# A guess of ScalarE and one Newton step for the quotients of a recurrence, in a decoder layer on one core

## The reference

```python
x = _layernorm(x + _L0_attn_ref(x, Wqkv, bqkv, Wo, bo))
x = _layernorm(x + _wkv(w, u, k=x, v=ctx))
x = _layernorm(x + _L0_ffn_ref(x, ...))      # (silu(g) * u) @ Wd.T

# _wkv, one step in time, for each batch row and channel
no = jnp.maximum(o, u + kt)
A = jnp.exp(o - no)
E = jnp.exp(u + kt - no)
y = (A * p + E * vt) / (A * q + E)
...
return ((A2 * p + E2 * vt, A2 * q + E2, no2), y)
```

## Time and profile before

| | us |
|---|---|
| three runs | 717.31, 719.03, 719.50 |
| their median | 719.03 |
| span of the profiled execution | 717.3 (the run of 717.31) |
| PE busy | 694.5 (97%) |
| DVE busy | 552.5 (77%) |
| ScalarE busy | 457.5 (64%) |
| GpSimd busy | 314.9 (44%) |

### The profile page before, as it was taken

How to read it: one execution, slowest core, us unless ns; L and a number is a source line. 1 busy time by engine, 2 the same in 40 slices (tenths; PEclk the granted TensorE clock), 3 DMA queues, 4 the chain that set the end, 5 groups by cost and what they waited for, 6 DMA issues and landing times. The chain is left out here.

```text
span 717.3 us, 13042 instructions
## 1 busy us (share of the span) xinstructions
PE 694.5 (97%) x4658; PEld 427.9 (60%) x4658; DVE 552.5 (77%) x1252; ACT 457.5 (64%) x1072; POOL 314.9 (44%) x352
## 2 busy tenths in 40 slices
PE   8899999999999999999999999999999799999997
PEld 3466665666666666656555454544455697578855
DVE  4567666879899988899945899998898786466644
ACT  5689885779887678768756744356552566346620
POOL 2015340455677342442345756576675243203321
PEclk9999999999999999999999999999999999999999
DMA  7846891343243043228026010000001000010001
GB/s 254 265 150 160 241 211 53 110 128 89 81 126 95 24 136 116 55 65 177 2 33 143 1 60 15 30 16 0 1 1 45 16 2 1 1 60 1 1 16 45
DMA packets 45538, 54.24 MB, mean 76 GB/s; under 512 B 4897, under 2 KB 34849, under 8 KB 45473
## 3 DMA queue, kind: packets, MB, share of 16 engines
q1 hardware_dynamic: 41632, 46.59, 21.2%
q0 software_dynamic: 3264, 6.29, 5.3%
q10 hardware_dynamic: 576, 0.52, 0.3%
HBM read 47.10 MB, written 12.58 MB: 83 GB/s over the span
## 5 line engine op out<-in xcount | busy, mean ns | idle before, releaser
L1422 DVE CUSTOM_DVE_ANT_0 ee<-psb,mask,clip 128x512 f32<-128x512 f32 (+3 forms) x256 | 131.1, 536 | 28.9 <-PE psb L974 28.3
L1201 ACT ACTIVATE ee<-ee,nm 128x512 f32<-128x512 f32 (+3 forms) x256 | 143.0, 561 | 1.4 <-DVE nm L1422 1.4
L1813 POOL TENSOR_TENSOR hl<-ring,hh 128x512 f16<-128x512 f32 x64 | 77.3, 1220 | 103.6 <-ACT hh L1315 61.3
L1212 ACT ACTIVATE ee<-psb 128x512 f32<-128x512 f32 (+1 forms) x172 | 87.1, 525 | 38.5 <-PE psb L985 33.4
L985 PE MATMUL psb<-ident,ee 128*128 128x128 f32 x640 | 97.6, 274 | 3.2 <-ACT ee L1212 3.0
L1110 PE MATMUL psb<-wd,hl 128*128 128x512 f16 x240 | 91.0, 379 | 0.6 <-POOL hl L1813 0.6
L1108 PE MATMUL psb<-wd,hh 128*128 128x512 f16 x240 | 91.0, 379 | 0.0
L985 PEld LDWEIGHTS psb<-ident,ee 128*128 128x128 f32 x640 | 75.6, 141 | 24.5 <-ACT ee L1212 6.0
L974 PE MATMUL psb<-ks,qs 128*128 128x512 f16 (+3 forms) x256 | 72.0, 301 | 2.7 <-DVE nm L1422 1.3
L1521 DVE RECIPROCAL ek<-ek 128x128 f32<-128x128 f32 x64 | 58.2, 931 | 6.5 <-POOL ek L1781 6.5
L932 PE MATMUL psb<-xh,wqk 128*128 128x512 f16 x240 | 59.8, 379 | 0.4 <-ACT wqk L1178 0.4
(11 more groups left out here) (205 smaller groups left out, 1614.4 us busy)
## 6 DMA issues: line engine op xcount, KB each, us to landing
qs<-parts SPq DMA_DIRECT2D x64, 128.0 KB, 2.8
ks<-parts SPq DMA_DIRECT2D x60, 128.0 KB, 3.0
parts<-qhl SPq DMA_DIRECT2D x16, 256.0 KB, 2.2
...
```

What stands on the lines that cost most here:

```text
L1201: e.activation(dst, dst, ACT.Exp, bias=NM[:, n % 4, col:col + 1], scale=-1.0, accum_out=DEN[:, n % 4, col:col + 1]).then_inc(sem("exp"), 1)
L1212: e.activation(ET[h][:, base:base + width], PSB[:, bank["turn", H, item], 0:width], ACT.Copy).then_inc(sem("et"), 1)
L1422: e.tensor_tensor_reduce(E[H % 3][:, EOFF[i]:EOFF[i] + w], PSB[:, bank["score", H, i], 0:w], MASK[:, S - w:S], -SC, CLIP[:, i:i + 1], ALU. ...
L1813: e.tensor_tensor(HS[it][1][:], pair(b, it // 2)[:, it % 2, :] if b in SEVEN else ring(b, it)[1], HS[it][0][:], ALU.subtract).then_inc(sem ...
```

## The change

A column has five pieces now, ek apart: scan_q, scan_p, seed, refine, divide.

- `seed`: ScalarE takes the logarithm of the denominator into a new buffer SEED (2 KB for each partition), then the exponential of minus that, in place. Both functions and the exponential of `ek` are in one table set, which `logs()` loads where the gate's function was used since.
- `refine`: GpSimd multiplies the denominator by the seed (r) and the numerator by the seed (s).
- `divide`: DVE makes (r - 2) x s in one operation of 128 x 512. It is the quotient after one Newton step with the sign turned; `r2` subtracts where it added.
- Before EKV is written DVE waits for `scan_p` of the column before. `chained` and the flushes keep the pieces of a column in their order: `ek` of a column has the whole of the column two before ahead of it, and the scans of the one before.
- The DMA scratch goes to 8192 bytes.
- All the numbers of the timetable that were placed by hand are placed anew. Outside the columns: product sums `WS_AT`, x2 turns of b = 2 a slot later, wo units among the gates (`WO_IN`), and `OH_POOL`, by which ScalarE makes the copy `oh` of 2 head groups where it made 8, GpSimd the others.

```diff
-WAIT = {..., 't1': 1, ..., 'scan_q': 2, 'scan_p': 7, 'divide': 8, ..., 'x2h': 0, ...}
-WAIT_IN = {..., 'scan_q': 1, 'scan_p': 1, 'divide': 2, ..., 'x2h': 0, ...}
+WAIT = {..., 't1': 0, ..., 'scan_q': 2, 'scan_p': 7, 'seed': 7, 'refine': 9, 'divide': 13, ..., 'x2h': 0, ...}
+WAIT_IN = {..., 'scan_q': 0, 'scan_p': 6, 'seed': 3, 'refine': 3, 'divide': 6, ..., 'x2h': 4, ...}
...
-          (2, 0): 266, (2, 1): 271, (2, 2): 274, (2, 3): 276, (3, 0): 283, (3, 1): 289, (3, 2): 291, (3, 3): 294}
+          (2, 0): 269, (2, 1): 271, (2, 2): 274, (2, 3): 278, (3, 0): 281, (3, 1): 289, (3, 2): 291, (3, 3): 294}
...
-WS_AT = {1: (276, 279), 2: (280, 283), 3: (276, 279), 4: (287, 291)}
+WS_AT = {1: (275, 282), 2: (280, 283), 3: (278, 282), 4: (291, 295)}
...
-OH_POOL = (1, 1, 1, 1, 1, 1, 0, 0, 0, 0, 0, 0, 1, 1, 0, 0)
+OH_POOL = (1, 1, 0, 1, 1, 1, 1, 1, 1, 0, 1, 1, 1, 1, 1, 1)
...
+    SEED = sb(ctx, "seed", [P, S], F32)
...
+        def logs():
+            if loaded[0] != "log":
+                e.preload_act_table_set("natural_log_exp_and_others")
+            loaded[0] = "log"
+
+        def seed(b, c):
+            z = T * b + c
+            logs()
+            act.wait_ge(sem("den"), z + 1)
+            if z:
+                act.wait_ge(sem("refine"), 2 * z)
+            e.activation(SEED[:], EK2S[c % 2][:], ACT.Ln).then_inc(sem("seed"), 1)
+            act.wait_ge(sem("seed"), 2 * z + 1)
+            e.activation(SEED[:], SEED[:], ACT.Exp, scale=-1.0).then_inc(sem("seed"), 1)
...
-            e.tensor_tensor(X[b][:, t, :], PSB[:, bank["yt", b, t], :], X[b][:, t, :], ALU.add).then_inc(sem("r2"), 1)
+            e.tensor_tensor(X[b][:, t, :], X[b][:, t, :], PSB[:, bank["yt", b, t], :], ALU.subtract).then_inc(sem("r2"), 1)
...
+                dve.wait_ge(sem("scan_p"), z)
                 e.tensor_tensor(EKV[:], EK[:], CTS[b][:, c, :], ALU.mult).then_inc(sem("ekv"), 1)
...
-        def divide(b, c, k):
-            cut = slice(k * P, (k + 1) * P)
-            dve.wait_ge(sem("den"), T * b + c + 1)
-            e.reciprocal(EK2S[c % 2][:, cut], EK2S[c % 2][:, cut]).then_inc(sem("rcp"), 1)
+        def divide(b, c):
+            dve.wait_ge(sem("refine"), 2 * (T * b + c) + 2)
+            e.scalar_tensor_tensor(out=CTS[b][:, c, :], in0=EK2S[c % 2][:], scalar=2.0, in1=CTS[b][:, c, :],
+                                   op0=ALU.subtract, op1=ALU.mult).then_inc(sem("y2"), 1)
...
-        def divide(b, c, k):
+        def refine(b, c):
             z = T * b + c
-            if k == T - 1:
-                pool.wait_ge(sem("num"), z + 1)
-                pool.wait_ge(sem("rcp"), 4 * z + 4)
-                e.tensor_tensor(CTS[b][:, c, :], CTS[b][:, c, :], EK2S[c % 2][:], ALU.mult).then_inc(sem("y2"), 1)
+            pool.wait_ge(sem("seed"), 2 * z + 2)
+            e.tensor_tensor(EK2S[c % 2][:], EK2S[c % 2][:], SEED[:], ALU.mult).then_inc(sem("refine"), 1)
+            pool.wait_ge(sem("refine"), 2 * z + 1)
+            pool.wait_ge(sem("num"), z + 1)
+            e.tensor_tensor(CTS[b][:, c, :], CTS[b][:, c, :], SEED[:], ALU.mult).then_inc(sem("refine"), 1)
...
-    nc = bacc.Bacc("TRN2", target_bir_lowering=False, num_devices=1)
+    nc = bacc.Bacc("TRN2", target_bir_lowering=False, num_devices=1, dynamic_dma_scratch_size=8192)
```

More of the change, by code:

```diff
@@ L75 @@
 LAST_AT = (5, 5, 6)
[L76 to L82, removed]
@@ L93 @@
[L93 to L96, removed]
-WS_AT = {1: (276, 279), 2: (280, 283), 3: (276, 279), 4: (287, 291)}
+WAIT = {'high': 1, 'low': 1, 'vtake': 1, 'r1': 2, 'norm': 6, 'exp': 4, 'eb': 0, 't1': 0, 't3': 0, 'oh': 2, 'ol':
+        3, 'ek': 1, 'scan_q': 2, 'scan_p': 7, 'seed': 7, 'refine': 9, 'divide': 13, 'r2': 3, 'x2h': 0, 'x2l': 3,
+        'expand': 0}
@@ new lines @@
+WAIT_IN = {'r1': 0, 'norm': 2, 'ek': 0, 'scan_q': 0, 'scan_p': 6, 'seed': 3, 'refine': 3, 'divide': 6, 'r2': 0,
+           'x2h': 4, 'x2l': 2, 'norm2': 5}
+PIECE_AT = {'load_second': 39, 'small': 81, 'split_wo': 46, 'load_ds': 180}
+WU_AT = (51, 52, 52, 52)
+WU_ZERO = (60, 124, 127, 142)
+WG_AT = (201, 222, 225, 228)
+WG_ZERO = (222, 230, 241, 244)
+REST_AT = (0, 22, 101, 10)
+BO_AT = (57, 102, 128, 173)
+XLOAD = {1: (0, 0, 18, 24), 2: (53, 58, 78, 85), 3: (136, 140, 157, 166)}
+XSPLIT = {1: (23, 26, 32, 38), 2: (84, 89, 91, 96), 3: (149, 149, 162, 169)}
@@ new lines @@
+WKV_AT = {(0, 0): 111, (0, 1): 123, (0, 2): 134, (0, 3): 144, (1, 0): 193, (1, 1): 207, (1, 2): 262, (1, 3): 264,
+          (2, 0): 269, (2, 1): 271, (2, 2): 274, (2, 3): 278, (3, 0): 281, (3, 1): 289, (3, 2): 291, (3, 3): 294}
+YT_AT = {0: (158, 166, 167, 179), 1: (268, 268, 269, 269), 2: (283, 284, 285, 288), 3: (299, 301, 301, 306)}
+X2_AT = {0: (223, 227, 229, 230), 1: (272, 274, 274, 274), 2: (293, 293, 293, 293), 3: (311, 313, 313, 313)}
+WO_IN = (10, 10, 11, 14)
+ZERO_IN = (5, 7, 7, 10, 10, 10, 11, 11, 12, 12, 13, 14, 14, 14, 14, 15)
@@ L300, in normed, with chained @@
                         late(WAIT["ol"], lambda: add("ol", n)))
+    CHAIN = ("scan_q", "scan_p", "seed", "refine", "divide")
+    def chained(b, c, last):
+        for name in CHAIN[:CHAIN.index(last) + 1]:
+            if (name, b, c) not in tt.place:
+                add(name, b, c)
     def wkv(b, c):
+        z = T * b + c
         def ek():
-            if b or c:
-                tt.flush(("divide", *divmod(T * b + c - 1, T), T - 1))
+            if z >= 2:
+                chained(*divmod(z - 2, T), "divide")
+            if z:
+                chained(*divmod(z - 1, T), "scan_p")
             add("ek", b, c)
+            for name in CHAIN:
+                late(max(wait(name) - wait("ek"), 0), lambda name=name: chained(b, c, name))
         tt.flush(("norm", 0, b, 0, T))
@@ L311, in wkv @@
         late(wait("ek"), ek)
-        late(wait("scan_q"), lambda: add("scan_q", b, c))
-        late(wait("scan_p"), lambda: add("scan_p", b, c))
-        for k in range(T):
-            late(wait("divide") + k, lambda k=k: add("divide", b, c, k))
     def yt(b, t):
@@ L324, in residual @@
                     add("load_ct", 2 * b + 1)
-        tt.flush(("divide", b, T - 1, T - 1))
+        for c in range(T):
+            if ("ek", b, c) not in tt.place:
+                tt.flush(("ek", b, c))
+            chained(b, c, "divide")
         tt.unit("yt", b, t)
@@ L1166, in _ @@
         act = Waiting(e)
+        loaded = [None]
         def split_x(b, k):
@@ L1305, in silu @@
         def silu(b, it):
+            loaded[0] = "gate"
             m, k = divmod(it, 2)
@@ L1374, in _ @@
                 out_norm(*a[1:3])
+            elif name == "seed":
+                seed(*a)
             elif name == "ek":
@@ L1848, in _ @@
                 scan_p(*a)
-            elif name == "divide":
-                divide(*a)
+            elif name == "refine":
+                refine(*a)
             elif name == "load_f":
```

22 lines of the change are left out of this document (9 added, 13 removed).

## The result

The changed kernel takes 738.63 us, median of four runs (736.68 to 740.88), against 718.33 before: a ratio of 1.028, interval 1.0252 to 1.0306. Forecast was 715.3, in a range of 710.5 to 720.0, with a chance of 0.14 for slower. It is 20 us slower.

A forecast was written before the change was run, and what follows sets the result against it. PE, busy 694.5 of 717.3 us, bounds the kernel, so only its waits can go. Gains 3.4 + 0.7 + 0.4 less costs 0.5 and 0.3 make 3.7; 719.03 - 3.7 = 715.3 us, range 710.5 to 720.

The forecast's parts named there:

- Attention, at nothing: Attention stage: order hardly moves and its largest waits are for ScalarE's copies, not reciprocals; no gain or cost.
- sign of being wrong: Stretch 24 to 350 us: shorter or longer by more than 2 us would show the forecast wrong.
- The start: Start of the kernel: a V part ahead of the score that waited 0.39 for DVE; gain 0 to 0.4, taken 0.4.
- The products, 3.4 gained: Seven products of batch 2, 548 to 565 us: PE waits less for snaps; gain 3.0 to 3.9 us, taken 3.4.
- the second wait: Second pair of batch 2's products: PE's stall of 3.2 to 3.3 us, at 561.45 before, goes.
- yt(1,0): Flip at 414 us: the quotient of (1,3) has no slack left; cost 0 to 3.8 us, taken 0.5.
- yt(0,0): Flip at 234 us: divide one slot ahead of it; cost 0 to 1, up to 2 us, taken 0.3.
- rival (1): Late quotient eats the gain: yt(1,0) and yt(0,0) cost 3 to 5 instead of 0.8; taken 718.5 us; chance 0.18.
- hl at y(0,0): PE's wait for hl at 436.72: column (2,0) moves back behind hl15; gain 0 to 0.7 us, taken 0.7.
- Rival (4): Each table switch holds ScalarE for twice its load: 5.1 us more in the chain to yt(1,0), 720.4; chance 0.03.
- Rival (2): Attention stage gains too from freed DVE time and fewer reciprocals between masks: 5.3 us more, 710; chance 0.12.
- Rival (3): Slower: GpSimd's multiplications at their long price of 2.06 at every flip; +2.8 us, 721.8; chance 0.13.

The follow-up runs named there:

- e_att_recip: Kernel before, reciprocals kept, with only the changed kernel's placing of the attention stage: 736.83 us, ratio 1.0248.
- e_qk: Changed kernel with only the projections of stacks 4 and 5 put back at slots 38, 44 and 45, 55: 729.47 us.
- e_seed: Changed kernel with only the seed of column (3,3) moved on ScalarE behind the third copy of the first pair of products: 734.59 us.
- e_bmoves: Kernel before, own start, reciprocals kept, with norms of y(1,2), y(1,3) moved behind the snaps and reciprocals of (3,3) behind c22 and second c11: 714.04 us.
- e_best3: Changed kernel with old attention places to slot 120 but new start, logarithm's table loaded first, and quotient pieces, norms, weight sums moved at its waits: 719.17 us.
- e_bfix: Kernel before, reciprocals kept, with the changed kernel's start and norms and reciprocals of (3,3) moved later at batch 2's products: 713.08 us.

## Why the prediction was wrong

- **Attention, at nothing.** This step failed first and cost most: 11 of 17.6 us. The prediction read that "the order of the attention stage hardly moves" on PE and did not follow what hangs on it. A projection six slots later made its write and the reads behind it 6.3 us later. It names wd as "the one load that GpSimd issues", where GpSimd issues those of wu and wg too, and it is the four of wu that had drawn together, just there. And bo met a norm. e_att_recip has this loss without any quotient, and e_qk takes 9.2 back with two entries of one table. Its own sign of being wrong, the stretch from 24 to 350 us longer by more than 2 us, came true. The start, taken at 0.4, gave 2.9: the first score starts 0.8 earlier, and about 1.5 is half clock (0.50 from 24.33 to 27.74, with 3.0 us of PE's work in it) that the trace after has not. All four traces read here that have the old start show that stretch, and one of the twelve with the new start. A late load of xt, for which PE waits 1.8 at 68.63, took 1.2 back at once.
- **The products, 3.4 gained.** The mechanism named was right in one half: the second wait of 3.2 went. The working error is one line. It let the denominator come at 550.2 (564.6 in the time of the run) and so let the norm of y(1,2) behind the seed cost nothing. GpSimd's rs and shift of y(1,2) stand ahead of c2 and took 0.94 and 1.73; the denominator came at 568.8. The prediction's own have it at 554.10 before, 3.9 later than its sum, and 3.9 is nearly the whole of what followed: the first wait, "stays", grew by 4.3. The half clock behind it, 2.6 us, was in no term. e_seed shows the queue to be the cause by moving the seed alone. Net: +3.2 where -3.4 was forecast, from the first product to the last.
- **yt(1,0), 0 to 3.8, taken 0.5.** 1.6. In the range by luck, since the way was another: GpSimd's numerator and refinement ran at 1.26 us there, and the delay was DVE behind ScalarE's th 11. yt(0,0), taken 0.3, was 0.4. The two together are 2.0, under the 3 to 5 of rival (1), and not by its cause.
- **Small gains.** hl at y(0,0): its wait is gone, as said.
- **What was not seen.** A table load inside attention, since its exponentials had used another set (1.1 us), and r2 behind the weight sum of WS_AT (1.4).
- **Prices.** Right: seed 0.63 each, multiplications 1.37 and 1.42, divide 0.87, scratch nothing. A switch of tables costs its load: 0.02 us around each, and the rows above. Rival (4) falls, and with it the 1380 ns of DRAIN that the Trainium skill gives ("ScalarE: Activation LUTs", What ACT_TABLE_LOAD costs).
- **Rival (2)** fell: no attention stall went with the freed DVE. **Rival (3)** had the side right and the mechanism wrong; the multiplications were short.
- **Slips in its sums**, without weight for the outcome: the costs of 3 to 5 in rival (1) give 717.5 to 719.5 and not "717.3 to 719", and 714 less half of rival (2) is 711.4, where the range begins at 710.5.
- **The deeper step** was to charge the second stall to the reciprocals' length. e_bmoves keeps them and gains 4 us, more than the forecast, by order alone. After the moves tried on each, the quotient (e_best3, 719.2) is 6 us behind the reciprocals (e_bfix, 713.1). By PE's starts 5.5 of 5.8 us of that arise at the products, and in attention e_best3 is as far ahead of the kernel before as e_bfix (2.4 and 2.2). A part of the gap may be a better place that was not tried, so it is not shown that the quotient must lose.
